# Attention on one Trainium2 core: weighted sums of two units in a row, and the row maxima spread anew

## The chip, the cores and the metric

The kernel runs on one core of a Trainium2 chip. Its time is the device time of one execution in microseconds (us); of several executions the median is told. Times inside an execution come from the hardware profiler and count from the start of the span. An engine's name stands for its queue: TensorE (PE, its weight loads PEld), VectorE (DVE), ScalarE (ACT), GpSimd (POOL), SyncE (SP, which issues the transfers). Instructions of one queue run in order; between queues there are semaphores only.

## The reference

Two layers on x of 2 x 1024 tokens and 512 features, in float32. Each layer is attention on the normalized input, gated by a feed-forward part. The change lies in layer 1:

```python
xn = layernorm(x)
q = rope((xn @ Wq.T) as 32 heads of 16);  k = rope((xn @ Wk.T) as 8 heads);  v = (xn @ Wv.T) as 8 heads
scores = einsum('bhgtd,bhkd->bhgtk', q, k) / sqrt(16)      # 4 query heads g share a key head h
scores = where(causal, scores, lowest)
ctx = einsum('bhgtk,bhkd->bhgtd', softmax(scores), v)
s = ctx @ Wo.T
w_gu, w_d = dequantized 4-bit weights
g = silu((silu(gate) * up) @ w_d)                           # gate, up = halves of xn @ w_gu
out = x + s * g
```

## The kernel before

Layer 0 runs first (to about 341 us), then layer 1: the weights Wq, Wk, Wv and the tokens are turned and split into high and low parts, projections and rope (to about 466 us), the feed-forward part (to about 860 us), attention (about 890 to 1389 us), output projection.

**Attention.** There are NG = 16 groups n (2 batches x 8 key heads), each with four query heads. Scores are made transposed (keys on partitions, queries along the row), in units (h, k): h is the half of 512 queries, k the block of 128 keys. `UNITS` has the 12 units of a group in their order: (0,0) to (0,3), then (1,0), (1,4) to (1,7), (1,1) to (1,3). A unit on the diagonal is narrower (512, 384, 256, 128 columns). Each unit has two half units c = 2i, 2i+1 (`NC` = 24 of them), each for two query heads:

- `scores(n, c)` on TensorE (line 1885): two matmuls into one of two score banks, `score_bank[c % 2]`, and so behind the exponential of c - 2.
- the exponential on ScalarE (line 1417) into `prob`. The buffer holds two units; for even c ScalarE first waits until the unit two earlier has been weighed (`av_done`).
- on the diagonal, a select on GpSimd (line 1298) clears what is masked.
- `weighed(n, i)` on TensorE (line 1901): the sum over keys of v times the exponentials of unit i, for four heads as 32-column tiles of the array, accumulated over the units of one h in the bank `sum_bank`. Float32 makes two passes of four matmuls of it. Before, it comes at every odd half unit: at c the unit c // 2 - 1, behind the first item of that half unit.

When one h is complete, ScalarE copies the sums (`turn`, line 1390), TensorE turns them (line 1909), VectorE normalizes them (lines 1649, 1651).

The exponentials need each row's maximum beforehand. For that there are 48 *items* per group, `ITEMS`: scores with queries on partitions (TensorE, line 1861, up to 512 keys), and a maximum over the row on VectorE: masked with an accumulator read behind it (line 1626) for the last piece of a row, plain (line 1629) for the others. An item needs one of three spare banks, and so waits until VectorE is done with the item or turn three places earlier (`freed`). Items of the next group run among the half units of this one; from c = 19 (`TURN_MAXIMA`) on there come "early" items of the group after the next. At c = 19 TensorE turns the maxima (line 1874), and SP brings them into the queries' spare rows for the next group.

The order is written out ahead of time: `beside(c)` deals the 48 items, by cost w + 96 for w columns, out to the 24 half units; `tasks` adds the turns (maxima at c = 19, the half h = 0 at c = 10, the group before's h = 1 at c = 2); `todo(n, c)` gives them their banks. TensorE's loop in each half unit: scores, the first task, a weighted sum if one is due, the other tasks. VectorE goes through the same list.

**The head of layer 1.** Four token tiles per chunk of 512 are normalized by ScalarE, turned by TensorE (`turn_tokens`) into `turn_bank(t)`, two banks in turn, rounded by ScalarE (`high_parts`) and subtracted by VectorE (`low_parts`); TensorE waits with tile t for the low part of t - 2. Then the projections of the chunk. Behind rope each piece of q and k is rounded (`round_rope`, ScalarE), its low part made (`low_rope`, VectorE, line 1564), and both are stored by SP, in three buffers.

**The start of the feed-forward part.** The weights of step s + 1 are dequantized by VectorE piece by piece while TensorE works on step s. For that SP loads packed weights (`quants`) and scales (`scales(s)`, semaphore `sz_in`, 32 per step), and TensorE spreads scales over partitions (`piece`). `values(c)` (VectorE, line 1569) copies the turned values out of a bank that the feed-forward part wants next; `h_ready` tells TensorE so.

Of the kernel before, what the change touches and what calls it, by code (L numbers as in the profile page):

```python
# [6 lines left out]
F32 = mybir.dt.float32  # L7
# [833 lines left out]
HG = G  # L841
# [30 lines left out]
def beside(c):  # L872


    cost = [w + 96 for *_, w in ITEMS]
    upto = lambda x: sum(sum(cost[:s + 1]) <= sum(cost) * x / NC + 1e-6 for s in range(len(ITEMS)))
    at = (c - TURN_MAXIMA) % NC
    return range(upto(at), upto(at + 1))
# [23 lines left out]
def layer1(nc, shared, Wo, qw_gu, qz_gu, sc_gu, gi_gu, qw_d, qz_d, sc_d, gi_d, rotate_d, cos_d, sin_d, shift_d,  # L902
# [10 lines left out]
    with ExitStack() as ctx:  # L913
# [53 lines left out]
        mx, mx_first = place(nc, "mx", [P, STACKS, 2, 2, QB], F32, 147), place(nc, "mx_first", [P, 2, 2, QB], F32, 147.375)  # L967
        prob, ctxt = place(nc, "prob", [P, 2, HG, CH], F32, 147.5), place(nc, "ctxt", [P, HALF, CH], F32, 163.5)
        rden = place(nc, "rden", [P, QPH, HG], F32, 167.5)
        ctx_sb = place(nc, "ctx_sb", [P, NG, QB, HG * D], F32, 48)  # L970

        wn = v_all[:, 0:KT * E // (QB * 2 * D)].rearrange("p n b d -> p (n b d)").rearrange("p (o e) -> p o e", o=KT)
        woh, wol = place(nc, "woh", [P, KT, E], F32R, 187.5), place(nc, "wol", [P, KT, E], F32R, 195.5)
        x1 = place(nc, "x1", [P, TILES, E], F32, 80)
# [38 lines left out]

        def turn_bank(t):
            return bank[:, t % 2]

# [77 lines left out]
        outv = out.rearrange("b (t p) e -> p (b t) e", p=P)  # L1094
        x1v = x1_d.rearrange("(c t p) e -> p c t e", p=P, t=TPC)

        block = ctx.enter_context(nc.Block())

        @block.sync
        def _(sp):  # L1100
# [93 lines left out]
            for c in range(CHUNKS):  # L1194
                b, u = c // 2, c % 2
                for m in range(ROT):
                    r = rope(c, m)
                    sp.wait_ge(ql_ready, r + 1)
                    if m < ROT - 1:
                        at = b * (HKV * G) + m * heads  # L1200
                        dst = q_scr[at:at + heads]
                    else:
                        dst = k_scr[b * HKV:b * HKV + HKV]
                    for n, part in enumerate((qh, ql)):
                        sp.dma_start(dst[:, n, :, u * CH:u * CH + CH], part[:, r % HALVES].bitcast(F32)).then_inc(q_out[r % HALVES], 16)
                    if r >= HALVES - 1:
                        stored(r - HALVES + 1)
                    if c == 0 and m == 3:
                        sp.wait_ge(s_out, 96)
                        scales(0)  # L1210
                    if c == 1 and m == 0:
                        reload(3)
                    if (c, m) in LOADS:
                        for n in LOADS[c, m]:
                            quants(0, n // 3, *PIECES[n % 3])
            scales(1)
            for r in range(CHUNKS * ROT - HALVES + 1, CHUNKS * ROT):
# [29 lines left out]
        def _(pool):  # L1247
# [44 lines left out]
            for n in range(NG):  # L1292
                for c in range(NC):
                    h, k = UNITS[c // 2]
                    if diagonal(h, k):
                        pool.wait_ge(exp_done, n * NC + c + 1)
                        p = prob[:, c // 2 % 2, c % 2 * 2:c % 2 * 2 + 2, span(h, k):span(h, k) + P]
                        pool.affine_select(out=p, in_=p, compare_op=ALU.is_ge, fill=0.0, base=0,  # L1298
                                           pattern=[[0, 2], [1, P]], channel_multiplier=-1).then_inc(masked, 1)
                    if c == HEAD and n + 1 < NG:  # L1300
                        if n > 0:
                            pool.wait_ge(av_done, n * NU)
                        values(n + 1)
                    if n == NG - 1 and c == HEAD + 1:
                        pool.wait_ge(st_ps, (NG - 1) * NC)
                        pool.wait_ge(ctx_ready, 2 * HKV)
                        context(0)
                        context(1)
# [6 lines left out]
        def _(act):  # L1315
# [10 lines left out]
            def high_parts(c, tiles):  # L1326
                for t in tiles:
                    at = (c * TPC + t) * P
                    act.wait_ge(tp_ready, c * TPC + t + 2)
                    act.activation(xth[:, :, at:at + P], turn_bank(t).rearrange("p (k q) -> p k q", k=KT),  # L1330
                                   ACT.Copy).then_inc(xth_ready, 1)
# [75 lines left out]
            for n in range(NG):  # L1407
                for c in range(NC):
# [3 lines left out]
                    if c == 2 * QPH + 2:  # L1412
                        turn(n, 0)
                    if c % 2 == 0 and n * NU + c // 2 >= 2:
                        act.wait_ge(av_done, n * NU + c // 2 - 1)
                    act.wait_ge(st_ps, n * NC + c + 1)
                    act.activation(prob[:, c // 2 % 2, c % 2 * 2:c % 2 * 2 + 2, lo:], score_bank[c % 2][:, :, lo:], ACT.Exp,  # L1417
                                   scale=D ** -0.5).then_inc(exp_done, 1)
# [12 lines left out]
        def _(dve):  # L1431
# [123 lines left out]
            def low_parts(c, tiles):  # L1555
                for t in tiles:
                    at = (c * TPC + t) * P
                    dve.wait_ge(xth_ready, c * TPC + t + 1)
                    dve.tensor_tensor(xtl[:, :, at:at + P], turn_bank(t).rearrange("p (k q) -> p k q", k=KT),
                                      xth[:, :, at:at + P].bitcast(F32), ALU.subtract).then_inc(xtl_ready, 1)  # L1560
# [19 lines left out]
            for c in range(CHUNKS):  # L1580
# [7 lines left out]
                for m in range(ROT):  # L1588
# [14 lines left out]
                    if (c, m) in MADE:  # L1603
# [4 lines left out]
                        if n == 2:  # L1608
                            pick(0, 1)
            low_rope(CHUNKS * ROT - 1)  # L1610
            values(CHUNKS - 1)
            dve.drain().then_inc(h_ready, 1)  # L1612
            dve.sem_inc(acc_ready, 1)
            each_pair(dve, body)
# [107 lines left out]
        def _(pe):  # L1722
# [84 lines left out]
            def turn_tokens(c, tiles):  # L1807
                for t in tiles:
                    pe.wait_ge(xn_ready, c * TPC + t + 1)
                    if t >= 2:  # L1810
                        pe.wait_ge(xtl_ready, c * TPC + t - 1)
                    elif t == 0 and c > 1:
                        pe.wait_ge(v_ready, c)
                    for k in range(KT):
                        mm = pe.transpose(turn_bank(t)[:, k * P:k * P + P], xb[:, c % 2, t, k * P:k * P + P], ident[:, :])
                    mm.then_inc(tp_ready, 1)
# [11 lines left out]
            for c in range(CHUNKS):  # L1828
                tokens = slice(c * CH, c * CH + CH)
                pe.wait_ge(xtl_ready, c * TPC + TPC)  # L1830
                for m in range(OT):
# [14 lines left out]
                    if (c, m) in ROWS:  # L1846
                        n = ROWS[c, m]
                        if n == 0:
                            pe.wait_ge(sz_in, 32)
                        piece(0, n // 3, *PIECES[n % 3])  # L1850
# [38 lines left out]
            def weighed(n, i):  # L1889
# [10 lines left out]
                for g in range(HG):  # L1900
                    mm = pe.matmul(sum_bank[2 * D * g:2 * D * (g + 1), lo:], vst[:, n % STACKS, k], prob[:, i % 2, g, lo:],  # L1901
                                   start=(k == 0), stop=(k == last))
# [70 lines left out]
            for n in range(NG):  # L1973
                for c in range(NC):
                    scores(n, c)
                    part = list(todo(n, c))
                    run(n, c, part[:1])
                    if c > 1 and c % 2 == 1:
                        weighed(n, c // 2 - 1)
                    elif c == 1 and n > 0:  # L1980
                        weighed(n - 1, NU - 1)
                    run(n, c, part[1:])
                    if n == NG - 1 and c in WO_STEPS:
                        turn_weights(WO_STEPS.index(c))
            turn_context(0)
            turn_context(1)
            weighed(NG - 1, NU - 1)
            project(0)
# [79 lines left out]
```

## Time and profile before

| | us |
|---|---|
| median of 3 runs (1449.43 to 1455.82) | 1450.42 |
| the profiled execution, its own time | 1447.45 |
| its span | 1445.7 |
| TensorE busy | 1333.2 (92%) |
| VectorE busy | 1059.5 (73%) |
| ScalarE busy | 618.3 (43%) |
| GpSimd busy | 334.8 (23%) |
| mean granted TensorE clock | 0.962 |

An engine's busy time is the union of its instructions. Matmuls overlap in the records (their ends are modelled), so the distance of two starts says more than a duration. In the chain of waits that ended last TensorE holds 64% of the span, VectorE 6%, ScalarE 2%; the largest lines in it are TensorE's 1861 (12%), the feed-forward matmuls 38 to 40 (9 to 10% each), 1901 (10%) and 1885 (9%).

### The profile page before, as it was taken

Reading aid. Unit: us, or ns where it says so; the run is one execution under the profiler, and the core shown is the slowest. Engines: PE = TensorE matmul, PEld = TensorE weight load, DVE = VectorE, ACT = ScalarE, POOL = GpSimd, SP = SyncE. Lnnn points to the kernel's source line nnn. Section 1 sums busy time; section 2 is a strip of 40 time slices with the busy share of each in tenths; the row PEclk is TensorE's granted clock in tenths of the full one; section 3 lists DMA queues with packets and bytes.
Section 4 is the critical chain, followed back from the end, with each engine's and each line's share of the span. In section 5 each row is a group of like instructions: output and inputs, shape, how many; then the busy total and the mean of one; then the engine's idle time right before and its main releaser. Section 6 shows DMA issues by size and latency. Waiting matters only on the chain.

```text
span 1445.7 us, 19982 instructions
## 1 busy us (share of the span) xinstructions
PE 1333.2 (92%) x6642; PEld 926.3 (64%) x6642; DVE 1059.5 (73%) x2495; ACT 618.3 (43%) x859; POOL 334.8 (23%) x387
## 2 busy tenths in 40 slices
PE   3788988995999999999999988999999999999898
PEld 2557675764766777777777764555555555555467
DVE  6887979697686555555554577888888888888457
ACT  4733755364442111111111112666666666666652
POOL 2653657363321000000000000221122222112221
PEclk9978998897999999999999996999999999999999
DMA  6102100024344100000000130111221132231002
GB/s 214 66 10 78 59 30 30 0 102 135 91 137 132 45 23 22 23 22 22 22 14 11 38 66 1 34 34 34 42 59 36 34 92 63 64 76 21 2 30 87
DMA packets 45021, 76.04 MB, mean 53 GB/s; under 512 B 9540, under 2 KB 16660, under 8 KB 44932
## 3 DMA queue, kind: packets, MB, share of 16 engines
q1 hardware_dynamic: 44628, 74.83, 18.5%
q8 instruction: 48, 0.79, 0.2%
q14 instruction: 41, 0.34, 0.1%
q10 hardware_dynamic: 304, 0.09, 0.0%
HBM read 55.60 MB, written 19.01 MB: 52 GB/s over the span
## 4 chain that ended last, share of the span: by engine, by line
PE 64%; DVE 6%; ACT 2%; issue 2%; DVEq 1%; POOL 1%; DMA 0%; POOLq 0%; SPq 0%; ACTq 0%
PE d_bank L1861 12%; PE d_bank L38 10%; PE d_bank L1901 10%; PE d_bank L40 9%; PE d_bank L39 9%; PE d_bank L1885 9%; PE d_bank L1909 1%; DVE mx_first L1629 1%; DVEq L1632 1%; DVE d_bank L1626 1%; DVE hl L1483 1%; PE d_bank L1738 1%; DVE hs L1478 1%; PE d_bank L1843 1%; ACT hh L1381 1%
## 5 line engine op out<-in xcount | busy, mean ns | idle before, releaser
L1417 ACT ACTIVATE prob<-d_bank 128x1024 f32<-128x1024 f32 (+3 forms) x384 | 302.4, 811 | 209.6 <-PE d_bank L1885 204.9
L1626 DVE CUSTOM_DVE_ANT_0 d_bank<-d_bank,mask 128x256 f32<-128x256 f32 (+3 forms) x512 | 255.0, 521 | 45.7 <-PE d_bank L1861 39.3
L1861 PE MATMUL d_bank<-kst,qst 96*128 96x512 f32 (+3 forms) x768 | 264.4, 386 | 5.2 <-DVE mx_first L1629 2.7
L1861 PEld LDWEIGHTS d_bank<-kst,qst 96*128 96x128 f32 x768 | 144.1, 193 | 143.7 <-DVE mx L1626 58.8
L1885 PE MATMUL d_bank<-qst,kst 98*128 98x512 f32 (+3 forms) x768 | 207.5, 353 | 0.5 <-ACT prob L1417 0.5
L1298 POOL TENSOR_SCALAR_AFFINE_SELECT prob<-prob 128x256 f32<-128x256 f32 x256 | 103.9, 407 | 447.0 <-ACT prob L1417 445.2
L1629 DVE TENSOR_REDUCE mx_first<-d_bank 128x1 f32<-128x512 f32 (+1 forms) x256 | 167.8, 655 | 21.1 <-PE d_bank L1861 14.5
L1901 PE MATMUL d_bank<-prob,vst 128*32 128x512 f32 (+3 forms) x1536 | 164.3, 500 | 1.1 <-POOL prob L1298 1.1
L1373 ACT ACTIVATE hs<-d_bank 128x512 f32<-128x512 f32 (+1 forms) x44 | 26.3, 598 | 299.8 <-PE d_bank L40 297.5
L38 PE MATMUL d_bank<-xtl,wgh 128*128 (+1 forms) x352 | 141.4, 402 | 2.7 <-DVEq L1612 2.5
L1885 PEld LDWEIGHTS d_bank<-qst,kst 98*128 98x128 f32 x768 | 130.3, 191 | 19.5 <-ACT prob L1417 8.2
L40 PE MATMUL d_bank<-xth,wgh 128*128 (+1 forms) x352 | 137.8, 391 | 0.0
L39 PE MATMUL d_bank<-xth,wgl 128*128 (+1 forms) x352 | 137.6, 391 | 0.0
L1478 DVE TENSOR_TENSOR hs<-hs,d_bank 128x512 f32<-128x512 f32 (+1 forms) x44 | 30.2, 687 | 103.4 <-ACT hs L1373 103.4
L1249 POOL COPY vst<-v_all 128x256 f32<-128x256 f32 x16 | 6.3, 396 | 362.3 <-DVE kst L1617 362.3
L266 POOL TENSOR_TENSOR pb<-at,qkv 128x2048 f32<-128x2048 f32 x16 | 73.5, 4591 | 69.6 <-DVE so L571 50.0
L257 POOL TENSOR_TENSOR pa<-qkv 128x2048 f32<-128x2048 f32 x16 | 73.1, 4568 | 55.8 <-DVE qkv L552 31.6
L38 PEld LDWEIGHTS d_bank<-xtl,wgh 128*128 128x128 f32 (+1 forms) x352 | 65.5, 186 | 26.6 <-issue 10.1
L38 PE MATMUL d_bank<-wdl,hh 128*128 128x512 f32 (+1 forms) x176 | 70.9, 403 | 4.9 <-DVE acc L1493 3.2
L40 PEld LDWEIGHTS d_bank<-xth,wgh 128*128 128x128 f32 (+1 forms) x352 | 65.6, 186 | 15.1
L38 PE MATMUL bank<-xtl,w1h 128*128 128x512 f32 x128 | 56.4, 441 | 19.7 <-DVE al L625 18.3
L39 PEld LDWEIGHTS d_bank<-xth,wgl 128*128 128x128 f32 (+1 forms) x352 | 65.7, 187 | 13.4
(265 smaller groups left out, 2419.2 us busy)
## 6 DMA issues: line engine op xcount, KB each, us to landing
wst<-L_ffn_w SPq DMA_DIRECT2D x8, 1024.0 KB, 6.5
qst<-q_scr SPq DMA_DIRECT2D x32, 256.0 KB, 4.6
qw<-L_ffn_qweight_gu SPq DMA_DIRECT2D x40, 128.0 KB, 2.6
xb<-x_d SPq DMA_DIRECT2D x4, 1024.0 KB, 7.4
q_scr<-qh SPq DMA_DIRECT2D x16, 256.0 KB
q_scr<-ql SPq DMA_DIRECT2D x16, 256.0 KB
kst<-k_scr SPq DMA_DIRECT2D x32, 128.0 KB, 3.6
qst<-q_scr SPq DMA_DIRECT2D x32, 128.0 KB, 4.9
```

The costliest lines, as they stand in the source:

```text
L38: pe.matmul(out, wh, ml, start=first, stop=False)
L39: pe.matmul(out, wl, mh, start=False, stop=False)
L40: return pe.matmul(out, wh, mh, start=False, stop=last)
L257: pool.tensor_tensor(pa[:, :, :, :], q, k, ALU.mult).then_inc(p1_done, 1)
L266: pool.tensor_tensor(pb[:, :, :, :], a, v, ALU.mult).then_inc(p2_done, 1)
L1298: pool.affine_select(out=p, in_=p, compare_op=ALU.is_ge, fill=0.0, base=0, pattern=[[0, 2], [1, P]], channel_multiplier=-1).then_inc(maske ...
L1417: act.activation(prob[:, c // 2 % 2, c % 2 * 2:c % 2 * 2 + 2, lo:], score_bank[c % 2][:, :, lo:], ACT.Exp, scale=D ** -0.5).then_inc(exp_d ...
L1626: dve.tensor_tensor_reduce(sc, sc, mask[:, CH - w:CH], 1.0, LEAST, ALU.add, ALU.max, mx[:, u, h % 2, h // 2, q:q + 1]).then_inc(spare_free, 1)
L1629: dve.tensor_reduce(mx_first[:, h % 2, h // 2, q:q + 1], sc, AX.X, ALU.max).then_inc(spare_free, 1)
L1861: pe.matmul(spare_bank(number)[:, 0:w], qst[u][0:M_ROW, h // 2, q * P:q * P + P], kst[u][0:M_ROW, h % 2, at:at + w], start=True, stop=True ...
L1885: mm = pe.matmul(score_bank[c % 2][:, hh_, lo:], kst[u][0:M_ROW + 2, hh_, k * P:k * P + P], qst[u][0:M_ROW + 2, c % 2, h * CH + lo:(h + 1) ...
L1901: mm = pe.matmul(sum_bank[2 * D * g:2 * D * (g + 1), lo:], vst[:, n % STACKS, k], prob[:, i % 2, g, lo:], start=(k == 0), stop=(k == last))
```

## The change

- `weighed` runs at c % 4 == 1 only, for two units, c // 2 - 2 and c // 2 - 1 (at c = 1 the last two of the group before). Two tasks stand ahead of it, the rest behind. After the last group the last two units are weighed, not the last one.
- The exponentials have a second buffer of two units: `prob(i)` is unit i's place among four, and ScalarE waits for the unit four earlier. `woh` and `wol` (Wo's parts, written in the last group) move to make room, onto the third buffers of queries and keys.
- `beside(c)` no longer gives each half unit an equal part of the items' cost, but 17 parts at c % 4 == 1 and 5 elsewhere. That makes 4 or 5 items at c % 4 == 1 and one or two elsewhere; of the early items 9, not 10, run ahead of the loop.
- Chunk 0's token tiles turn into four banks; tiles 2 and 3 wait for low parts of the weights (`w_lo`), no longer for a low part of the tokens.
- `scales(1)` is issued by SP right behind `scales(0)`, in chunk 0, and the first piece waits for both.
- At the end of the projections VectorE does `values` and `h_ready` first, and the last `low_rope` behind them.

```diff
     cost = [w + 96 for *_, w in ITEMS]
-    upto = lambda x: sum(sum(cost[:s + 1]) <= sum(cost) * x / NC + 1e-6 for s in range(len(ITEMS)))
+    share = [17 if (at + TURN_MAXIMA) % 4 == 1 else 5 for at in range(NC)]
+    upto = lambda x: sum(sum(cost[:s + 1]) <= sum(cost) * sum(share[:x]) / sum(share) + 1e-6 for s in range(len(ITEMS)))
...
-        prob, ctxt = place(nc, "prob", [P, 2, HG, CH], F32, 147.5), place(nc, "ctxt", [P, HALF, CH], F32, 163.5)
+        probs = [place(nc, f"prob{i}", [P, 2, HG, CH], F32, at) for i, at in enumerate((147.5, 187.5))]
...
-        woh, wol = place(nc, "woh", [P, KT, E], F32R, 187.5), place(nc, "wol", [P, KT, E], F32R, 195.5)
+        woh, wol = place(nc, "woh", [P, KT, E], F32R, 171.5), place(nc, "wol", [P, KT, E], F32R, 179.5)
...
-        def turn_bank(t):
-            return bank[:, t % 2]
+        def turn_bank(c, t):
+            return bank[:, t if c == 0 else t % 2]
...
+        def prob(i):
+            return probs[i // 2 % 2][:, i % 2]
...
                         scales(0)
+                        scales(1)
...
-            scales(1)
...
-                    if c % 2 == 0 and n * NU + c // 2 >= 2:
-                        act.wait_ge(av_done, n * NU + c // 2 - 1)
+                    if c % 2 == 0 and n * NU + c // 2 >= 4:
+                        act.wait_ge(av_done, n * NU + c // 2 - 3)
...
-            low_rope(CHUNKS * ROT - 1)
             values(CHUNKS - 1)
             dve.drain().then_inc(h_ready, 1)
+            low_rope(CHUNKS * ROT - 1)
...
-                    if t >= 2:
+                    if t >= 2 and c == 0:
+                        pe.wait_ge(w_lo, t - 1)
+                    elif t >= 2:
                         pe.wait_ge(xtl_ready, c * TPC + t - 1)
...
-                            pe.wait_ge(sz_in, 32)
+                            pe.wait_ge(sz_in, 64)
...
                     scores(n, c)
                     part = list(todo(n, c))
-                    run(n, c, part[:1])
-                    if c > 1 and c % 2 == 1:
-                        weighed(n, c // 2 - 1)
-                    elif c == 1 and n > 0:
-                        weighed(n - 1, NU - 1)
-                    run(n, c, part[1:])
+                    run(n, c, part[:2])
+                    if c % 4 == 1:
+                        for i in (c // 2 - 2, c // 2 - 1):
+                            if i >= 0 or n > 0:
+                                weighed(n if i >= 0 else n - 1, i % NU)
+                    run(n, c, part[2:])
...
+            weighed(NG - 1, NU - 2)
             weighed(NG - 1, NU - 1)
```

## Rows read from the trace of the kernel before

**Rows 1.** Windows, one group: length, busy us (instructions) by engine, clock, DMA, GB/s.
```profile
983.45:1014.85 31.40, 30.90 (x206) 18.08 (x206) 27.28 (x87) 19.88 (x27) 6.85 (x17) 1.00 0.20 39
```

**Rows 2.** Timeline, TensorE around a weighted sum: start, us, engine, line, operation, tiles, shapes.
```profile
1014.49 0.40 PE L1861 MATMUL d_bank<-kst,qst 96*128 96x512 f32 x1
1014.82 1.06 PE L1901 MATMUL d_bank<-prob,vst 128*32 128x512 f32 x8
...
1015.27 0.61 PE L1901 MATMUL d_bank<-prob,vst 128*32 128x512 f32 x4
1015.82 0.45 PE L1861 MATMUL d_bank<-kst,qst 96*128 96x384 f32 x1
1016.10 0.63 PE L1885 MATMUL d_bank<-qst,kst 98*128 98x512 f32 x2
1016.56 0.64 PE L1861 MATMUL d_bank<-kst,qst 96*128 96x512 f32 x2
```

**Rows 3.** Timeline, scores and exponentials; in brackets idle time before, and its releaser.
```profile
1007.45 0.64 PE L1885 MATMUL d_bank<-qst,kst 98*128 98x512 f32 x2
...
1008.18 1.94 ACT L1417 ACTIVATE prob<-d_bank 128x1024 f32<-128x1024 f32 x2 [1.43 <-PE d_bank L1885]
...
1383.02 1.02 ACT L1417 ACTIVATE prob<-d_bank 128x1024 f32<-128x1024 f32 x1
...
1384.09 0.50 PE L1885 MATMUL d_bank<-qst,kst 98*128 98x512 f32 x1 [0.16 <-ACT prob L1417]
```

**Rows 4.** Timeline, VectorE in half units 0 to 5 of a group.
```profile
1016.30 0.57 DVE L1626 CUSTOM_DVE_ANT_0 d_bank<-d_bank,mask 128x384 f32<-128x384 f32 x1 [0.56 <-PE d_bank L1861]
...
1020.09 0.73 DVE L1626 CUSTOM_DVE_ANT_0 d_bank<-d_bank,mask 128x512 f32<-128x512 f32 x1
...
1021.31 0.42 DVE L1651 TENSOR_TENSOR ctx_sb<-d_bank,rden 128x256 f32<-128x256 f32 x1
1021.87 0.56 DVE L1629 TENSOR_REDUCE mx_first<-d_bank 128x1 f32<-128x384 f32 x1
1022.34 0.42 DVE L1626 CUSTOM_DVE_ANT_0 d_bank<-d_bank,mask 128x256 f32<-128x256 f32 x1
...
1022.68 0.69 DVE L1629 TENSOR_REDUCE mx_first<-d_bank 128x1 f32<-128x512 f32 x1
1023.28 0.42 DVE L1626 CUSTOM_DVE_ANT_0 d_bank<-d_bank,mask 128x256 f32<-128x256 f32 x1
```

**Rows 5.** Timeline, an item that waits for its bank.
```profile
1005.97 0.14 DVE L1626 DVE_READ_ACCUMULATOR2_ANT mx<- 128x1 f32 x1
...
1006.17 0.50 PE L1861 MATMUL d_bank<-kst,qst 96*128 96x512 f32 x1
```

**Rows 6.** Timeline, the last item's accumulator read and the maxima's transpose.
```profile
1009.57 0.14 DVE L1626 DVE_READ_ACCUMULATOR2_ANT mx<- 128x1 f32 x1
...
1010.12 0.27 PE L1874 MATMUL d_bank<-ident,mx 128*32 128x128 f32 x1 [0.37 <-DVE mx L1634]
```

**Rows 7.** Timeline, the head of layer 1.
```profile
351.63 1.29 DVE L1559 TENSOR_TENSOR xtl<-d_bank,xth 128x512 fp32r<-128x512 f32 x2 [2.03 <-ACT xth L1330]
...
355.49 0.77 PE L38 MATMUL d_bank<-xtl,wth 128*128 128x512 f32 x1 [1.61 <-DVE xtl L1559]
```

**Rows 8.** Timeline at the feed-forward part's start, and below it one window (columns as rows 1).
```profile
466.82 0.50 PE L38 MATMUL d_bank<-xtl,wgh 128*128 x1 [2.47 <-DVEq L1612]
...
468.13 1.33 SPq L1125 DMA_DIRECT2D zz<-z_gu_scr  x1
...
472.34 0.47 PE L1738 MATMUL d_bank<-sz,hot 8*128 8x512 f32 x1 [2.50 <-issue]
...
475.91 0.49 DVE L1462 TENSOR_SCALAR wq<-qw,lane_shift 128x512 uint32<-128x512 uint32 x1 [3.20 <-DMA qw<-L_ffn_qweight_gu]
...
479.40 0.68 DVE L1478 TENSOR_TENSOR hs<-hs,d_bank 128x512 f32<-128x512 f32 x1
...
473.00:476.40 3.40, 3.40 (x9) 2.69 (x9) 0.49 (x1) 0.00 (x0) 0.00 (x0) 0.52 0.46 134
```

More of the change, by code:

```diff
@@ L967, in layer1 @@
         mx, mx_first = place(nc, "mx", [P, STACKS, 2, 2, QB], F32, 147), place(nc, "mx_first", [P, 2, 2, QB], F32, 147.375)
-        prob, ctxt = place(nc, "prob", [P, 2, HG, CH], F32, 147.5), place(nc, "ctxt", [P, HALF, CH], F32, 163.5)
+        probs = [place(nc, f"prob{i}", [P, 2, HG, CH], F32, at) for i, at in enumerate((147.5, 187.5))]
+        ctxt = place(nc, "ctxt", [P, HALF, CH], F32, 163.5)
         rden = place(nc, "rden", [P, QPH, HG], F32, 167.5)
@@ L1296, in _ @@
                         pool.wait_ge(exp_done, n * NC + c + 1)
-                        p = prob[:, c // 2 % 2, c % 2 * 2:c % 2 * 2 + 2, span(h, k):span(h, k) + P]
+                        p = prob(c // 2)[:, c % 2 * 2:c % 2 * 2 + 2, span(h, k):span(h, k) + P]
                         pool.affine_select(out=p, in_=p, compare_op=ALU.is_ge, fill=0.0, base=0,
@@ L1329, in high_parts @@
                     act.wait_ge(tp_ready, c * TPC + t + 2)
-                    act.activation(xth[:, :, at:at + P], turn_bank(t).rearrange("p (k q) -> p k q", k=KT),
+                    act.activation(xth[:, :, at:at + P], turn_bank(c, t).rearrange("p (k q) -> p k q", k=KT),
                                    ACT.Copy).then_inc(xth_ready, 1)
@@ L1413, in _ @@
                         turn(n, 0)
-                    if c % 2 == 0 and n * NU + c // 2 >= 2:
-                        act.wait_ge(av_done, n * NU + c // 2 - 1)
+                    if c % 2 == 0 and n * NU + c // 2 >= 4:
+                        act.wait_ge(av_done, n * NU + c // 2 - 3)
                     act.wait_ge(st_ps, n * NC + c + 1)
-                    act.activation(prob[:, c // 2 % 2, c % 2 * 2:c % 2 * 2 + 2, lo:], score_bank[c % 2][:, :, lo:], ACT.Exp,
+                    act.activation(prob(c // 2)[:, c % 2 * 2:c % 2 * 2 + 2, lo:], score_bank[c % 2][:, :, lo:], ACT.Exp,
                                    scale=D ** -0.5).then_inc(exp_done, 1)
@@ L1558, in low_parts @@
                     dve.wait_ge(xth_ready, c * TPC + t + 1)
-                    dve.tensor_tensor(xtl[:, :, at:at + P], turn_bank(t).rearrange("p (k q) -> p k q", k=KT),
+                    dve.tensor_tensor(xtl[:, :, at:at + P], turn_bank(c, t).rearrange("p (k q) -> p k q", k=KT),
                                       xth[:, :, at:at + P].bitcast(F32), ALU.subtract).then_inc(xtl_ready, 1)
@@ L1814, in turn_tokens @@
                     for k in range(KT):
-                        mm = pe.transpose(turn_bank(t)[:, k * P:k * P + P], xb[:, c % 2, t, k * P:k * P + P], ident[:, :])
+                        mm = pe.transpose(turn_bank(c, t)[:, k * P:k * P + P], xb[:, c % 2, t, k * P:k * P + P], ident[:, :])
                     mm.then_inc(tp_ready, 1)
@@ L1900, in weighed @@
                 for g in range(HG):
-                    mm = pe.matmul(sum_bank[2 * D * g:2 * D * (g + 1), lo:], vst[:, n % STACKS, k], prob[:, i % 2, g, lo:],
+                    mm = pe.matmul(sum_bank[2 * D * g:2 * D * (g + 1), lo:], vst[:, n % STACKS, k], prob(i)[:, g, lo:],
                                    start=(k == 0), stop=(k == last))
```

## The prediction, made before the changed kernel ran

> **What bounds the kernel now.** I read the page's chain first: TensorE holds most of it, and the costliest lines of it are the row maxima's scores (line 1861), the scores (1885) and the weighted sums (1901), so the attention loop is the stage to look at. The table of windows comes next: one group of the loop lasts 31.40 us, TensorE is busy for 30.90 of it at the full clock, VectorE for 27.28, ScalarE for 19.88 [rows 1]. TensorE ends nearly every step, but VectorE has only 4 us to spare per group, and that is where the argument turns. Then the timelines of single half units, for what a change of shape costs on TensorE, and for the distances between engines.
>
> A weighted sum uses the array as 32-column tiles, all else 128 columns. An item of 512 columns just ahead of one takes 0.33 us (1014.49 to 1014.82), where a 512 matmul otherwise takes 0.23 (two in 0.46 from 1016.10). The first pass of the unit takes 0.45, the second 0.55 until the next item starts, so leaving costs 0.10, and that item of 384 then takes 0.28 instead of about 0.175 (0.23 scaled by columns) [rows 2]. In and out together: 0.10 + 0.09 + 0.10 = 0.29 us, twelve times a group.
>
> **What the change takes away.** Two units back to back leave six of these twelve: 6 x 0.29 = 1.74 us a group, if nothing waits. No unit follows another directly in the trace; between its two passes nothing is lost, so I take 0 inside a pair, and 0.29 at worst. Unit costs, from 0.45 a pass scaled by columns: 512 0.91, 384 0.69, 256 0.48, 128 0.27.
>
> The Trainium skill has a reason for this cost (TensorEngine Tiling (Array Packing), Key Properties): changing the tiling mode drains the array. TensorE: Matmul & The Clock Gate (Step-by-step: what each phase is for) puts a drain at about 128 cycles, so, as an estimate, a pair of switches at 0.11 us, not 0.29; by that the sum below would come out 6 x 0.18 us a group higher, about 1491. The rows decide, because they hold the weight load too, which after a switch isn't hidden.
>
> **What the change adds.** A unit now comes only at every fourth half unit, and lasts twice as long. Three distances decide what happens between.
> Scores to exponentials: scores of 512 start at 1007.45, their exponential at 1008.18, so 0.73 later; it lasts 1.02, two of them 1.94, so 0.92 apart; scores two half units on start 0.05 after its end (1383.02 + 1.02, 1384.09) [rows 3]. There are two score banks before and after, so half unit c waits for the exponential of c-2. Before, two half units hold four items and a unit, 2.6 us, more than two exponentials. Now half units without a unit hold two scores and one or two items, 0.46 + about 0.25 = 0.71, less than 0.92: TensorE must wait.
> Items to VectorE: an item starts on VectorE 0.48 us after its matmul (384: 1015.82, then 1016.30 in the rows); there they last 0.34 (256), 0.47 (384), 0.60 (512), and a masked 512 with the normalization behind it 1.78 (1020.09 to 1021.87) [rows 4]. A masked 512 alone I take at 0.62, a 128 at 0.23 with 0.33 to its start (estimates, scaled). The masked form ends with an accumulator read of 0.14; 0.06 after it, the item three places on may start (1006.11, 1006.17) [rows 5], for there are three banks. During a pair VectorE gets nothing new: it works off three items at most and idles, and has to make up for it in the half units between.
> The maxima's transpose comes 0.55 after the last item's accumulator read starts (1009.57, 1010.12) [rows 6].
>
> **One group after, step by step.** I cut it where TensorE leaves a pair; there VectorE and ScalarE have run dry, so each block of four half units starts fresh. Times from the leave.
> Half units 22, 23, 0, 1 (all 512): two items 0.46; scores 22 start, exponential at 1.19, two of them end at 1.19 + 1.94 = 3.13; scores 1 start 3.18; + 0.46 + items 0.46 + 0.09 + pair 1.82 + 0.09 = 6.10.
> 2 to 5: VectorE sets it: first item at 0.33, then 0.23, 0.34, 0.47, 1.78, 0.47, 0.34 for the masked 256 of half unit 3, 0.14 + 0.06: the last item ahead of the pair starts at 4.16; + 0.33 + 1.60 + 0.09 = 6.18.
> 6 to 9: VectorE frees the bank of half unit 7's second item at 0.48 + 0.47 + 0.69 + 0.06 = 1.70, that item and scores 8 take it to 2.28, the next item waits until 2.37; + 0.18, scores 9 0.46, two items 0.41 + 0.09, pair 0.75 + 0.09 = 4.35.
> 10 to 13: the turned half puts scores 11 back to 1.56; their exponential starts 2.38, ends 3.40; scores 13 start 3.45; + 0.35 + 0.46 + 0.09 + 1.82 + 0.09 = 6.26.
> 14 to 17: as 2 to 5, without normalization: 0.33 + 0.23 + 0.34 + 0.47 + 0.62 + 0.47 + 0.34 + 0.20 = 3.00; + 0.33 + 1.17 + 0.09 = 4.59.
> 18 to 21: the maxima's transpose at 0.48 + 0.47 + 0.60 + 0.62 + 0.55 = 2.72; scores 20 until 3.29, item 0.18, scores 21 0.46, items 0.41 + 0.09, pair 1.17 + 0.09 = 5.69.
> Sum 33.17, against 31.40: 1.77 us more a group. Thirteen groups are of this kind: +23.0. The first (half clock at its start), the last but one (no early items) and the last (no items) I take at +1.0 each: ScalarE's wait is in them too, VectorE's mostly not; +3.0.
> Four kept units of exponentials cost nothing: their buffer was emptied by a pair one block earlier. That frees ScalarE from a wait that it doesn't have on the path now. Wo's halves, placed elsewhere, are written when those buffers are dead. The second last unit of the last group moves behind the loop, where the last one stood already: its switches go too, within 0.3 us either way.
>
> **The three small waits.** Four turning banks: TensorE starts the projections at 355.49, behind the last low part; two low parts take 1.29, so four without a pause end at 351.63 + 2.58 = 354.2 [rows 7]. TensorE follows 0.2 later: 1.1 us less; 0 to 1.1, and I take 1.1, for the stage is TensorE's after that.
> The values ahead of the last low part, and the scales loaded early, remove TensorE's waits of 2.47 before 466.82 and 2.50 before 472.34. But its next piece needs the product that VectorE makes at 479.40, behind the piece whose weights land at 475.91, and those stand behind the stores of q and k, which don't move. TensorE then waits there instead, 4 to 5 us. I take 0. The bounds: at best 0.2; at worst the wait puts the clock down: after the two waits it stood at 0.52 for 3.4 us [rows 8], which behind 480 would cost 1.7. The two loads on SP's queue (1.33 for the longer one at 468.13 [rows 8]) now stand ahead of the q stores of chunk 0; at most 2.7 us, taken as 0, because those stores have three buffers.
>
> **Sum.** The profiled execution took 1447.45 us (span 1445.7): + 23.0 + 3.0 - 1.1 = 1472.4. The median of the runs shown is 3.0 above it: 1475.
>
> **Rivals.**
> All waits stay hidden (0.09): only switches go, 15 x 1.74 + 1.1 = 27 us less, 1423, faster. For it: TensorE is at 98% of the group [rows 1], so whatever it saves shows. Against: TensorE's queue is in order, and with two score banks and three item banks nothing lets it run past the two distances above. It decides if the half units between pairs take TensorE more than 0.92 us; by the rows they take 0.71.
> Only ScalarE's wait shows, VectorE keeps up (0.05): 31.40 - 1.74 + 0.82 + 0.60 (what 6.10 and 6.26 stand above TensorE's own 5.28 and 5.66) = 31.1 a group, with the 1.1 about 1445.
> Only VectorE's shows (0.05): 33.17 - 1.42 = 31.75, about 1455.
> A pair saves nothing inside (0.03): + 1.74 a group, about 1500.
> The forecast: 0.78.
>
> **How the numbers follow.** 0.1 us in a block is 0.6 a group and 8 us in all, so the forecast alone spans 1465 to 1487. The range goes down to 1444 to take in the two middle cases, and up to 1488. What a measurement can tell from no change is about 0.5%, 7 us: faster 0.10, within 0.10, slower 0.80.
>
> **What would show it.** Right: the distance between leaves goes from 31.40 to about 33 us a group; scores (1885) wait for ScalarE in half units 0, 1 and 13; items (1861) wait for VectorE in 3 to 5, 7, 8 and 15 to 17; a pair of 512 takes 1.9 us; VectorE idles about 1 us in each pair; layer 1's first projection starts 1.1 us sooner against the turn; TensorE idles 4 us before 480. Wrong: a group under 31 us, or scores that don't wait.

## The result, and the profile after

The changed kernel takes 1480.37 us (median of four runs, 1479.3 to 1482.02), beside 1451.93 for the kernel before (four runs, 1449.43 to 1455.82): ratio 1.0194, interval 1.0167 to 1.0222. It is slower by 28.4 us; forecast were 1475 us, from terms that add up to 24.9.

The page of the changed kernel: the chain's shares first, then three of the costliest groups (after the bar: busy us, mean ns, then the idle time just before them and what ended it). Below them are the same three groups from the page of the kernel before.

```profile
PE 56%; DVE 10%; ACT 5%; issue 2%; DVEq 1%; DMA 1%; POOL 0%; SPq 0%; POOLq 0%; ACTq 0%
...
L1633 DVE CUSTOM_DVE_ANT_0 d_bank<-d_bank,mask 128x256 f32<-128x256 f32 (+3 forms) x512 | 254.6, 521 | 83.8 <-PE d_bank L1870 76.7
L1870 PE MATMUL d_bank<-kst,qst 96*128 96x512 f32 (+3 forms) x768 | 263.6, 392 | 13.5 <-DVE mx_first L1636 6.4
L1894 PE MATMUL d_bank<-qst,kst 98*128 98x512 f32 (+3 forms) x768 | 212.0, 360 | 11.3 <-ACT prob L1424 11.1
```

```profile
L1626 DVE CUSTOM_DVE_ANT_0 d_bank<-d_bank,mask 128x256 f32<-128x256 f32 (+3 forms) x512 | 255.0, 521 | 45.7 <-PE d_bank L1861 39.3
L1861 PE MATMUL d_bank<-kst,qst 96*128 96x512 f32 (+3 forms) x768 | 264.4, 386 | 5.2 <-DVE mx_first L1629 2.7
L1885 PE MATMUL d_bank<-qst,kst 98*128 98x512 f32 (+3 forms) x768 | 207.5, 353 | 0.5 <-ACT prob L1417 0.5
```

In the chain TensorE went from 64% to 56%, VectorE from 6% to 10%, ScalarE from 2% to 5%. TensorE's idle time ahead of scores rose from 0.5 to 11.3 us, nearly all of it ended by the exponential; ahead of items from 5.2 to 13.5. VectorE's masked maxima do the same 255 us of work, and VectorE stands idle ahead of them for 83.8 us where it was 45.7, nearly all of it ended by TensorE. ScalarE's idle time ahead of the exponentials went from 209.6 to 223.3 us. So all three engines wait more: they wait for one another in turn.

One group of the loop, answering to [rows 1] (a table of windows):

```profile
994.81:1028.21 33.40, 31.61 (x202) 18.68 (x201) 26.86 (x86) 19.82 (x26) 6.79 (x17) 1.00 0.18 36
```

It was 31.40 us long with TensorE busy for 30.90; now 33.40 and 31.61, so 1.8 us of it are idle instead of 0.5. The clock is full in both. Where the difference of the two profiled executions lies, by the start of the same instruction:

| place | before | after | difference |
|---|---|---|---|
| layer 1's first weight turn | 343.08 | 346.50 | +3.4 |
| first projection | 355.49 | 357.89 | +2.4 |
| last rope matmul | 457.32 | 460.29 | +3.0 |
| second piece of step 1's scales | 480.33 | 482.98 | +2.65 |
| first piece of step 2's scales | 509.75 | 513.95 | +4.2 |
| first scores of attention | 889.20 | 892.54 | +3.3 |
| last weighted sum | 1389.57 | 1423.24 | +33.7 |
| span | 1445.7 | 1479.6 | +33.9 |

The first line lies in front of everything that was changed: layer 0's code is the same, and over the kernels below it is 0 to 7.7 us longer than in the profile of before. Attention holds 30.3 us, the head of layer 1 and the feed-forward part together next to nothing.

A pair of weighted sums of 512 columns, half unit 1, answering to [rows 2, 4] (timeline: start, duration, engine, line):

```profile
995.40 0.63 PE L1870 MATMUL d_bank<-kst,qst 96*128 96x512 f32 x2
...
995.96 1.92 PE L1910 MATMUL d_bank<-prob,vst 128*32 128x512 f32 x16
...
997.05 0.14 DVE L1633 DVE_READ_ACCUMULATOR2_ANT mx<- 128x1 f32 x1
...
997.81 0.68 PE L1870 MATMUL d_bank<-kst,qst 96*128 96x128 f32 x3
...
998.18 0.30 DVE L1633 CUSTOM_DVE_ANT_0 d_bank<-d_bank,mask 128x128 f32<-128x128 f32 x1 [0.98 <-PE d_bank L1870]
```

The pair takes 1.85 us (995.96 to 997.81; forecast 0.91 + 0.91 + 0.09), so nothing is lost between its units. VectorE does its last item until 997.2 and then stands still for 0.98: it has nothing left, and will be missed afterwards. Those misses, with ScalarE's, answering to [rows 3, 5, 6], in the changed kernel's timeline:

```profile
1000.98 0.50 PE L1870 MATMUL d_bank<-kst,qst 96*128 96x512 f32 x1 [0.23 <-DVE ctx_sb L1658]
...
1005.85 0.39 PE L1870 MATMUL d_bank<-kst,qst 96*128 96x256 f32 x1 [0.22 <-DVE mx_first L1636]
...
1022.13 0.27 PE L1883 MATMUL d_bank<-ident,mx 128*32 128x128 f32 x1 [0.64 <-DVE mx L1641]
...
1026.24 3.90 ACT L1424 ACTIVATE prob<-d_bank 128x1024 f32<-128x1024 f32 x4 [1.34 <-PE d_bank L1894]
...
1027.41 0.70 PE L1894 MATMUL d_bank<-qst,kst 98*128 98x512 f32 x2 [0.44 <-ACT prob L1424]
```

Between two pairs TensorE waits for VectorE (the first three rows: half units 4 and 7, and the maxima's transpose), or for ScalarE (the last one: scores of half unit 0, while four exponentials run without a pause).

The head of layer 1 and the start of the feed-forward part, answering to [rows 7, 8] (timeline, then a table of windows):

```profile
355.15 2.48 DVE L1566 TENSOR_TENSOR xtl<-d_bank,xth 128x512 fp32r<-128x512 f32 x4 [2.16 <-ACT xth L1337]
...
357.89 0.77 PE L38 MATMUL d_bank<-xtl,wth 128*128 128x512 f32 x1 [2.54 <-DVE xtl L1566]
...
471.82 0.49 PE L1745 MATMUL d_bank<-sz,hot 8*128 8x512 f32 x1 [1.74 <-DVE hs L1485]
...
482.98 0.47 PE L1745 MATMUL d_bank<-sz,hot 8*128 8x512 f32 x1 [3.16 <-DVE hs L1485]
```

```profile
480.00:483.40 3.40, 0.42 (x2) 0.29 (x2) 2.39 (x4) 0.55 (x1) 0.00 (x0) 1.00 0.21 77
483.40:487.00 3.60, 3.60 (x10) 2.61 (x9) 2.93 (x6) 0.08 (x1) 0.00 (x0) 0.53 0.02 5
```

The four low parts of the tokens now run in one stretch. The wait of 2.47 us [rows 8] is gone and that of 2.50 is 1.74, but another of 3.16 stands at 483; behind it TensorE is granted 0.53 of its clock over 3.6 us.

### The profile page after: what moved, and what is told of

Read it like the earlier page. It is cut to its first block, busy times and chain, and to the rows that moved or that the text cites. A ratio compares the mean times of both kernels' runs of the same rounds, so it can differ in the third digit from the quotient of the medians.

```text
span 1479.6 us, 19980 instructions
## 1 busy us (share of the span) xinstructions
PE 1348.3 (91%) x6642; PEld 940.0 (64%) x6642; DVE 1052.7 (71%) x2495; ACT 617.2 (42%) x859; POOL 334.0 (23%) x387
## 4 chain that ended last, share of the span: by engine, by line
PE 56%; DVE 10%; ACT 5%; issue 2%; DVEq 1%; DMA 1%; POOL 0%; SPq 0%; POOLq 0%; ACTq 0%
PE d_bank L38 10%; PE d_bank L1870 9%; PE d_bank L1910 9%; PE d_bank L39 9%; PE d_bank L40 9%; PE d_bank L1894 7%; ACT prob L1424 4%; DVE d_bank L1633 3%; DVE mx_first L1636 2%; DVEq L1639 1%; PE d_bank L1918 1%; DVE hl L1490 1%; DVE hs L1485 1%; PE d_bank L1745 1%; PE d_bank L1852 1%
## 5 line engine op out<-in xcount | busy, mean ns | idle before, releaser
L1424 ACT ACTIVATE prob<-d_bank 128x1024 f32<-128x1024 f32 (+3 forms) x384 | 298.9, 809 | 223.3 <-PE d_bank L1894 221.3
L1633 DVE CUSTOM_DVE_ANT_0 d_bank<-d_bank,mask 128x256 f32<-128x256 f32 (+3 forms) x512 | 254.6, 521 | 83.8 <-PE d_bank L1870 76.7
L1870 PE MATMUL d_bank<-kst,qst 96*128 96x512 f32 (+3 forms) x768 | 263.6, 392 | 13.5 <-DVE mx_first L1636 6.4
L1894 PE MATMUL d_bank<-qst,kst 98*128 98x512 f32 (+3 forms) x768 | 212.0, 360 | 11.3 <-ACT prob L1424 11.1
L1870 PEld LDWEIGHTS d_bank<-kst,qst 96*128 96x128 f32 x768 | 138.9, 194 | 117.7 <-DVE mx L1633 55.4
L1380 ACT ACTIVATE hs<-d_bank 128x512 f32<-128x512 f32 (+1 forms) x44 | 26.3, 598 | 297.9 <-PE d_bank L40 295.6
L1910 PE MATMUL d_bank<-prob,vst 128*32 128x512 f32 (+3 forms) x1536 | 144.6, 494 | 0.0
L1910 PEld LDWEIGHTS d_bank<-prob,vst 128*32 128x32 f32 x1536 | 39.5, 109 | 67.3 <-issue 41.0
```

The lines of the kernel that those rows point to most:

```text
L1424: act.activation(prob(c // 2)[:, c % 2 * 2:c % 2 * 2 + 2, lo:], score_bank[c % 2][:, :, lo:], ACT.Exp, scale=D ** -0.5).then_inc(exp_done, 1)
L1633: dve.tensor_tensor_reduce(sc, sc, mask[:, CH - w:CH], 1.0, LEAST, ALU.add, ALU.max, mx[:, u, h % 2, h // 2, q:q + 1]).then_inc(spare_free, 1)
L1870: pe.matmul(spare_bank(number)[:, 0:w], qst[u][0:M_ROW, h // 2, q * P:q * P + P], kst[u][0:M_ROW, h % 2, at:at + w], start=True, stop=True ...
L1894: mm = pe.matmul(score_bank[c % 2][:, hh_, lo:], kst[u][0:M_ROW + 2, hh_, k * P:k * P + P], qst[u][0:M_ROW + 2, c % 2, h * CH + lo:(h + 1) ...
```

## The experiments

Loop times are told by the cut of the prediction, from where TensorE leaves the weighted sum of half unit c = 1, 5, 9, ... to where it leaves the next of these (distances of starts, us, an inner group):

| half units | before | forecast | after | e2 | e3 | e4 | e6 | e7 | e8 |
|---|---|---|---|---|---|---|---|---|---|
| 22 to 1 | 5.68 | 6.10 | 6.15 | 5.62 | 5.52 | 5.68 | 5.50 | 6.15 | 5.94 |
| 2 to 5 | 5.43 | 6.18 | 6.34 | 5.67 | 5.33 | 5.20 | 6.33 | 5.40 | 6.66 |
| 6 to 9 | 4.17 | 4.35 | 4.40 | 4.64 | 3.84 | 4.11 | 4.40 | 3.88 | 4.43 |
| 10 to 13 | 6.17 | 6.26 | 6.09 | 6.13 | 5.66 | 5.87 | 5.87 | 6.10 | 7.07 |
| 14 to 17 | 4.14 | 4.59 | 4.78 | 4.58 | 3.99 | 4.08 | 4.77 | 4.19 | 4.98 |
| 18 to 21 | 5.82 | 5.69 | 5.66 | 5.45 | 5.12 | 5.12 | 5.66 | 5.51 | 5.96 |
| group | 31.40 | 33.17 | 33.41 | 32.10 | 29.46 | 30.08 | 32.54 | 31.22 | 35.04 |

**e1, the three small waits alone** (in the kernel before; the main lines; the waits for `w_lo` and for both loads of scales are those of the changed kernel):

```diff
-            return bank[:, t % 2]
+            return bank[:, t if c == 0 else t % 2]
...
                         scales(0)
+                        scales(1)
...
-            low_rope(CHUNKS * ROT - 1)
             values(CHUNKS - 1)
             dve.drain().then_inc(h_ready, 1)
+            low_rope(CHUNKS * ROT - 1)
...
```

> Only the three small waits of layer 1 on the kernel before; attention untouched. Theory: the first projection comes 1.1 us sooner after the turns, the two waits before the feed-forward part move to the next piece, where TensorE stands idle 4 to 5 us and the clock falls to half behind it, 1.6 us lost; sum within 2 us of no change, attention groups 31.40. Rival: the waits were on the path and go, 1.1 + 2.5 + 2.5 = about 6 us faster.

1449.58 us against 1452.47, ratio 0.9989, interval 0.9976 to 1.0003. From layer 1's start the first projection comes 0.8 us sooner, and the piece at 510 only 0.3. Not all that lies between is the edit's: from the first projection to the last rope matmul e1 takes 99.3 us and the kernel before 101.8, but e10 and e5, whose code is the same up to there, take 102.4 and 99.3. Counted from the last rope matmul the piece at 480 comes 0.2 us sooner (23.0 to 22.8), and the one at 510 comes 2.9 us later (52.4 to 55.4). e1's timeline and window show why:

```profile
478.76 0.58 PE L1738 MATMUL d_bank<-sz,hot 8*128 8x512 f32 x1 [3.29 <-DVE hs L1478]
```

```profile
478.97:485.80 6.83, 6.83 (x16) 4.86 (x16) 3.58 (x6) 0.27 (x1) 0.00 (x0) 0.50 0.01 2
```

The removed waits return as one of 3.29 us, and the half clock behind it, for 6.8 us, makes the loss. The rival, 6 us faster, is out. The same stretch from the last rope matmul to 510 takes 53.7 to 56.2 us in the seven kernels here with this edit (53.7 in the changed one), and 52.2 to 52.4 in the five without.

**e2, the uneven items without pairs** (the changed kernel with one weighted sum at each odd half unit, still behind two tasks; after the last group one unit is left, as before the change):

```diff
-                    if c % 4 == 1:
-                        for i in (c // 2 - 2, c // 2 - 1):
-                            if i >= 0 or n > 0:
-                                weighed(n if i >= 0 else n - 1, i % NU)
+                    if c % 2 == 1 and (c > 1 or n > 0):
+                        weighed(n if c > 1 else n - 1, (c // 2 - 1) % NU)
...
```

> The changed kernel with one weighted sum at each odd half unit again, items still dealt 17 to 5. Theory (the pairs make ScalarE's and VectorE's waits): worked through as in the prediction the blocks come to 5.57, 5.47, 4.50, 5.95, 4.26, 5.46, a group of 31.2, about 1450 us. Rival (the uneven items make the waits): a group stays near 33.4, about 1480 us.

1460.95 us, ratio 1.0075, interval 1.0051 to 1.0099; a group 32.10, between the two. Without pairs the uneven items cost 0.7 us a group, the pairs on top of them 1.3. In the 0.7 is also that the sum stands behind two tasks, not one; the two were not separated. My steps came to 31.2, 0.9 too low.

**e3 and e4, lighter ScalarE and VectorE, after and before.** Both kernels take the exponential of only one of a half unit's two heads, and the item's maximum over 128 columns only; the diagonal's select is left out for the other head, and the weighted sums read the first one twice (lines of e3, the two main ones):

```diff
-                    act.activation(prob(c // 2)[:, c % 2 * 2:c % 2 * 2 + 2, lo:], score_bank[c % 2][:, :, lo:], ACT.Exp,
+                    act.activation(prob(c // 2)[:, c % 2 * 2:c % 2 * 2 + 1, lo:], score_bank[c % 2][:, 0:1, lo:], ACT.Exp,
...
-                    dve.tensor_reduce(mx_first[:, h % 2, h // 2, q:q + 1], sc, AX.X, ALU.max)
+                    dve.tensor_reduce(mx_first[:, h % 2, h // 2, q:q + 1], sc[:, 0:P], AX.X, ALU.max)
...
```

> The changed kernel with ScalarE and VectorE lightened in attention: the exponential is made for the first of two heads only (the weighted sums read that one twice), and an item's maximum is taken over 128 columns only. Theory: both waits go and only the saved switches are left, a group of 28.5 to 29.2, 15 x 4.5 below the changed kernel, about 1413 us. Rival (a pair costs TensorE itself): a group stays above 31, over 1445 us.

> The kernel before with the same two lightenings. Theory: TensorE bounds it already, only the waits at the maxima's and the sums' turns shrink: a group of 30.2 to 30.7, about 1437 us, and the light changed kernel lies 6 x 0.29 = 1.7 us a group below it, 24 to 28 us in all. Rival (switches are worth less, 0.11 a pair of them): the two differ by 0.7 a group, 10 us.

1413.07 us (ratio 0.9739, interval 0.972 to 0.9757) and 1415.07 (0.9755, 0.9736 to 0.9774). One group of each (windows; after first):

```profile
972.55:1002.01 29.46, 29.31 (x203) 18.69 (x202) 15.70 (x86) 12.86 (x27) 4.97 (x17) 1.00 0.20 41
```

```profile
971.40:1001.48 30.08, 30.08 (x203) 18.10 (x202) 16.66 (x86) 12.95 (x26) 5.05 (x17) 1.00 0.20 41
```

With the two engines light the changed loop is the shorter one: the loss hangs on their work. But it is shorter by 0.62 us a group, not by 1.74: the rival's number. Only two stretches save nearly a pair of switches each (6 to 9: 0.27; 10 to 13: 0.21), the one from 2 to 5 even loses 0.13. The distances of TensorE's starts tell more. From the matmul ahead of a weighted sum to the second start behind it, less 0.23 us per 512 columns for the matmul ahead and the one behind, TensorE takes 11.96 us a group in e4 and 9.87 in e3. So fewer switches save 2.1 us a group, 0.35 for each pair of them, and the rival's price of 0.11 is out. But 1.5 us come back among the other items, scores and turns, 0.2 of it ahead of the maxima's transpose; the pages note only 0.1 us a group of idle time more there, and what makes the rest is not shown.

Set against the heavy kernels, light engines save 3.95 us a group after the change and 1.32 before: 2.6 us of the loss go with ScalarE's and VectorE's work, which is more than the 2.1 that the pairs save. e4's total was also 22 us under what was expected, 10 of it ahead of the loop, where items run too.

**e6 and e7, one engine light at a time** (the changed kernel; e6 with e3's first edit, e7 with its second):

> The changed kernel with the exponential taken of the first head of a half unit alone (the weighted sums read it for both heads, and the causal select is on one head; output not the reference's); items and VectorE untouched. Theory: two separate waits were added, ScalarE's in half units 0, 1 and 13, VectorE's in the others. ScalarE's alone goes: the blocks that end in half units 1 and 13 fall from 6.15 and 6.09 to about 5.4 and 5.7, the other four stay within 0.2: group 33.41 to about 32.2, total about 1461. Rival 1 (VectorE is the one bound): within 0.3 us a group of 33.41, 1476 or more. Rival 2 (ScalarE is the one bound): group at 30 or below, 1430.

> The changed kernel with VectorE's part of every item cut to its last or first 128 columns (output not the reference's); exponentials untouched. Theory: VectorE's wait goes, ScalarE's stays: blocks that end in half units 1 and 13 stay at about 6.1 and 6.1, those that end in 5, 9, 17 and 21 fall from 6.34, 4.40, 4.78, 5.66 to about 5.3, 3.9, 4.0, 5.3: group about 30.7, total about 1440 (some us less if the items ahead of the loop get shorter too). Rival 1 (ScalarE is the one bound): group within 0.3 of 33.41. Rival 2 (one bound, VectorE): blocks that end in 1 and 13 fall as well, group 29.5 or below.

1465.75 us (ratio 1.0099, interval 1.0077 to 1.012) and 1441.24 (0.9928, 0.9906 to 0.995). The table shows the two waits apart. e6 shortens the stretches that end in half units 1 and 13, by 0.65 and 0.22, and no other by more than 0.01; e7 leaves just these two where they were and shortens the other four, by 0.94, 0.52, 0.59 and 0.15. The pages say the same, e6's first, then e7's (idle time behind the second bar):

```profile
L1870 PE MATMUL d_bank<-kst,qst 96*128 96x512 f32 (+3 forms) x768 | 267.2, 395 | 13.4 <-DVE mx_first L1636 6.4
L1894 PE MATMUL d_bank<-qst,kst 98*128 98x512 f32 (+3 forms) x768 | 208.3, 356 | 1.6 <-ACT prob L1424 1.2
```

```profile
L1870 PE MATMUL d_bank<-kst,qst 96*128 96x512 f32 (+3 forms) x768 | 240.0, 377 | 1.6 <-DVE mx_first L1636 0.7
L1894 PE MATMUL d_bank<-qst,kst 98*128 98x512 f32 (+3 forms) x768 | 219.3, 369 | 11.7 <-ACT prob L1424 11.4
```

Each lightening ends one kind of wait and leaves the other as it was (13.5 and 11.3 in the changed kernel). Alone they save 0.87 and 2.19 us a group, together (e3) 3.95. In the stretch from 18 to 21 it is 0, 0.15 and 0.54, and those from 10 to 13 and from 14 to 17 save 0.2 more together than apart: there each wait seems to cover part of the other.

**e8, pairs with even items:**

```diff
-    share = [17 if (at + TURN_MAXIMA) % 4 == 1 else 5 for at in range(NC)]
+    share = [1] * NC
```

> The changed kernel with the items spread evenly over the half units, as before the change, and the pairs left where they are. Theory (the time per half unit between pairs is what runs short, and the uneven shares, 17 with a pair and 5 without, put VectorE's work where TensorE is slow): the half units between pairs get about two more items for VectorE to work off while no pair runs, and the steps worked out as in the prediction give blocks of about 5.9, 6.7, 4.3, 7.7, 5.0, 5.9: group about 35.6, total about 1512, slower than the changed kernel. Rival (the uneven shares are what costs, pairs are nearly free): group below 33.4, total below 1480.

1514.25 us, ratio 1.044, interval 1.0421 to 1.046; a group 35.04. The uneven shares cost 0.7 us without pairs (e2), but with pairs they save 1.6: they are the remedy for the pairs, not the harm. Every second or third group is 1.6 us longer yet; e8's windows and timeline show why, for the same pair of half unit 5 in two groups:

```profile
1008.26:1011.41 3.15, 3.15 (x18) 0.60 (x17) 1.05 (x3) 0.00 (x0) 0.41 (x1) 0.50 0.00 0
1044.91:1046.55 1.64, 1.64 (x17) 0.42 (x17) 1.04 (x3) 0.00 (x0) 0.41 (x1) 1.00 0.00 0
```

```profile
1006.25 0.49 PE L1870 MATMUL d_bank<-kst,qst 96*128 96x512 f32 x1 [0.23 <-DVE ctx_sb L1658]
1006.95 0.39 PE L1870 MATMUL d_bank<-kst,qst 96*128 96x256 f32 x1 [0.20 <-DVE mx_first L1636]
...
1042.90 0.50 PE L1870 MATMUL d_bank<-kst,qst 96*128 96x512 f32 x1 [0.23 <-DVE ctx_sb L1658]
1043.59 0.39 PE L1870 MATMUL d_bank<-kst,qst 96*128 96x256 f32 x1 [0.19 <-DVE mx_first L1636]
```

One pair runs at 0.50 of the clock (1.2 GHz) and takes 3.15 us, the other at 1.00 (2.4 GHz) and takes 1.64, behind the same waits. Six of the groups have it, and in one of them a pair in half unit 13 too: some 12 of the 63 us. What decides between the two was not tried.

**e5 and e9, only small pairs, items as before.** The kernel before with the four turning banks and the four-unit buffers; `WEIGHED` lists the units weighed at each c (e5's is shown; e9 has `7: ()` and `9: (2, 3)` in it as well):

```diff
+        WEIGHED = {c: () for c in range(NC)} | {1: (-1,), 3: (0,), 5: (1,), 7: (2,), 9: (3,), 11: (4,), 13: (5,), 15: (6,), 17: (), 19: (7, 8), 21: (9,), 23: (10,)}
...
-                    if c > 1 and c % 2 == 1:
-                        weighed(n, c // 2 - 1)
-                    elif c == 1 and n > 0:
-                        weighed(n - 1, NU - 1)
+                    for i in WEIGHED[c]:
+                        if i >= 0 or n > 0:
+                            weighed(n if i >= 0 else n - 1, i % NU)
...
```

> The kernel before with the four turning banks and the four-unit buffers, every weighted sum alone in its old place but for units 7 and 8 (256 and 128 columns), which go together at half unit 19. Theory (a pair costs what the half units around it then wait; here the pair is the smallest one, 0.75 us, and stands where the maxima's transpose has just made TensorE wait anyway): from the leave of half unit 15 to the maxima's transpose VectorE ends it after the items of half units 16 and 17, now without the weighted sum of 17 between: 4.55 us instead of the 4.93 with it, so 0.4 us less a group, 6 over the loop, and up to 1.1 less from the banks: about 1445, ratio 0.995. Rival (any pair leaves the half units before it too short for ScalarE and VectorE): the group gets longer by 0.3 or more, 1455 or above.

> The kernel of e5 with a second small pair: units 2 and 3 (256 and 128 columns) together at half unit 9, all else alone. Theory (a pair pays only where TensorE waits for VectorE anyway, as ahead of the maxima's transpose; ahead of half unit 9 it doesn't): the stretch from the weighted sum of half unit 5 to that of 9 was 4.17 us in the kernel before and 4.40 and 4.43 in the two kernels with this pair, so about 0.25 more a group than e5: 31.4, total about 1449. Rival (each small pair saves its switches): 0.3 less than e5, 30.85, about 1441.

e5 takes 1445.05 us, ratio 0.9959, interval 0.9943 to 0.9975; e9 1442.35, 0.9941, 0.9918 to 0.9965. Both beat both kernels; the intervals of the two overlap, so neither is the better. A group of e5 and one of e9 (windows):

```profile
1016.44:1047.58 31.14, 30.86 (x203) 18.11 (x202) 27.09 (x88) 19.90 (x26) 6.85 (x17) 1.00 0.19 40
```

```profile
984.05:1015.22 31.17, 30.78 (x203) 18.16 (x202) 27.00 (x88) 20.14 (x27) 6.84 (x17) 1.00 0.20 41
```

e5's pair saves 0.25 us a group (0.38 expected): the stretch from half unit 15 to 19 grows from 4.17 to 4.32, the next, to 21, falls from 3.61 to 3.21, since VectorE gets the last items sooner and TensorE hardly waits for the maxima any more:

```profile
1040.33 0.14 DVE L1631 DVE_READ_ACCUMULATOR2_ANT mx<- 128x1 f32 x1
...
1040.89 0.27 PE L1881 MATMUL d_bank<-ident,mx 128*32 128x128 f32 x1
```

(0.56 apart, as 0.55 in [rows 6], but no idle time is noted ahead of the transpose, where it was 0.37.) e9's second pair does neither what the theory nor what the rival said: its stretch, from half unit 5 to 9, grows by 0.31 as expected (4.17 to 4.48), but the next one, to 11, gives 0.28 back (3.57 to 3.29). It is worth nothing, and costs nothing.

**e10, the turning banks alone:**

```diff
-            return bank[:, t % 2]
+            return bank[:, t if c == 0 else t % 2]
...
-                    if t >= 2:
+                    if t >= 2 and c == 0:
+                        pe.wait_ge(w_lo, t - 1)
+                    elif t >= 2:
...
```

> The kernel before with the four turning banks of layer 1 alone. Theory: the first projection comes 1.1 us sooner against the turns, nothing ahead of piece 5 changes and so no clock is lost there: the attention loop's groups stay at 31.40, the time at 0.5 to 1.1 us under the kernel before, and e5's gain of 6 us is the loop's but for this. Rival (e5's gain is the banks'): 4 us or more under the kernel before.

1449.08 us, ratio 0.9991, interval 0.9975 to 1.0006; the groups are 31.40 long, the first projection is 1.1 us sooner against the start of layer 1. From the first scores to the last weighted sum e5 and e9 take 496.7 and 496.5 us; the kernel before, e1 and e10 take 500.4 to 501.4. So about 4 of e5's 6 us are the loop's (0.25 us a group); the rest is the banks' and what runs differ by. The stretches without a pair are as long in e5 as before, so the four-unit buffer costs nothing there.

## Why the prediction was right

The mechanism held: pairs save their switches, and two separate waits, bound by the two score banks and the three item banks, give back more (2.6 against 2.1 us a group). Another 1.5 us a group come back with light engines too, which I had no term for. Term by term:

- *The switches*, 1.74 us a group: about 2.1, by e3 and e4, so 0.35 for each pair of switches instead of 0.29. Nothing was lost inside a pair. The Trainium skill (TensorEngine Tiling (Array Packing), Key Properties) has a drain at each change of mode; the trace agrees that a change costs something, but not with the 0.11 us estimated from the drain in TensorE: Matmul & The Clock Gate (Step-by-step: what each phase is for).
- *The blocks*, sum 33.17: 33.41. [22 to 1], [6 to 9] and [18 to 21] were within 0.05. [2 to 5] and [14 to 17], both VectorE's, came out 0.16 and 0.19 longer: masked maxima one behind another took 0.39 and 0.51 us (256 and 384 columns; lines below the list), where the prediction has 0.34, read ahead of a plain maximum, and 0.47, read from a plain one [rows 4]; and the item ahead of the pair took 0.42 instead of 0.33. [10 to 13] came out 0.17 shorter, for scores 11 start 1.41 us behind the leave and not 1.56 (1008.54, 1009.95). That the misses go both ways helped the sum, which is luck. 13 groups made +26.3 instead of +23.0.
- *Which engine ends which block*: ScalarE in 1 and 13, VectorE in the others, as e6 and e7 showed. The weakest step was [10 to 13]: there ScalarE holds only 0.22 us, and the block was no longer than before.
- *The three edge groups*, +3.0: the first +2.0, the last but one +1.95, the last +0.04. Together +4.0; the first two are like the inner ones after all, and the last, without items, loses nothing.
- *The turning banks*, -1.1: -1.0 in the profile (from +3.4 to +2.4), -1.1 in e10.
- *The two other waits*, 0 with bounds -0.2 and +1.7: +1.2 here (from +3.0 to +4.2 between the last rope matmul and 510). The bound at half the clock was the nearer one, not my 0: TensorE waited 3.16 us at 483 (4 to 5 expected) and then ran at 0.53. In the other kernels with this edit it cost up to 3.8, more than the bound. At the first scores of attention the difference is down to +3.3 again.
- *The rivals*: all waits hidden (1423) and only ScalarE's or only VectorE's wait (1445, 1455) fall with e6 and e7: each took one of the two waits away, and the other stood as before. That a pair saves nothing inside (1500) falls with the pair of 1.85 us.

Masked maxima one behind another, at the start of [14 to 17] (the changed kernel's timeline of VectorE):

```profile
1015.21 0.47 DVE L1633 CUSTOM_DVE_ANT_0 d_bank<-d_bank,mask 128x256 f32<-128x256 f32 x1
...
1015.60 0.60 DVE L1633 CUSTOM_DVE_ANT_0 d_bank<-d_bank,mask 128x384 f32<-128x384 f32 x1
...
1016.11 0.73 DVE L1633 CUSTOM_DVE_ANT_0 d_bank<-d_bank,mask 128x512 f32<-128x512 f32 x1
```

The sum was 1472.4 for a profiled execution and came out at 1481.3. Of the 8.9 us missing, 3.3 are the inner groups, 1.0 the edges, 1.2 the start of the feed-forward part, and 3.4 layer 0, which the change doesn't touch; what the other places differ by, under 1 us each, adds up to nothing. The median missed the forecast by 5.4 us only: layer 0's 3.4 lies within what single executions differ by (the profiled one before was 3.0 under its median then, the changed one 0.9 over).

## What to carry to other kernels

Putting two pieces of one kind together saves a switch, but it also takes away the work that lay between two dependent steps of other engines: count what is left there against their time per step, and against the buffers between. In this loop the one pair that paid (e5) stands where TensorE waited for another reason anyway. A wait removed ahead of a step that is late for its own reason came back behind it here, and the longer stand-still cost clock as well.

## What the runs showed of the hardware

- A stand-still of TensorE of 3.16 us (changed kernel) and 3.29 us (e1), at the same place, was followed by half the clock (1.2 GHz), for 3.4 us in the one and 6.8 in the other. In e10 the wait there is 1.40 us, and the clock behind it is full.
- In e8 waits of no more than 0.23 us each ahead of a pair of half unit 5 were followed by 0.50 of the clock in six groups and by 1.00 in eight others.
- Layer 0, the same code in all kernels, ended up to 7.7 us later in one profiled run than in another.
